# Interleaving two channels' lag weights in HBM, and making three of 32 chunks on chip instead of six

## The reference, cut to what matters

```python
# attention: r = layernorm(x); k = v = context
ek = exp(k)
A_t, B_t = sum over i<t of ew**(t-1-i) * ek_i * v_i, and the same without v   # ew = exp(w), per channel
#          the same again backwards, over i>t;  cur = exp(u + k)
wkv = (Af + Ab + cur * v) / (Bf + Bb + cur)
x = x + tanh(g_xattn) * sigmoid(r) * wkv
# feed-forward: z = layernorm(x), fake-quantised with one scale over all of z
h = fake_quant(silu(z @ quant(w_gate).T) * (z @ quant(w_up).T))
x = x + tanh(g_ffn) * h @ quant(w_down).T
```

## Time and profile before

| | |
|---|---|
| median of 3 timed runs | 212.69 us (212.09 to 212.9) |
| the profiled execution's own time | 211.43 us |
| its span, first to last instruction | 209.7 us |
| busy share of the span: PE, PEld | 82%, 60% |
| busy share: DVE, ACT, POOL | 80%, 75%, 66% |
| chunk products, line 1019 (PE) | 512 MATMUL, 60.4 us busy, 280 ns mean |
| DMA moved in all | 29.31 MB in 43328 packets |
| of these lag loads | 26 transfers of 512 KB, 7.3 us from issue to landing (median) |

### The profile page before, as it was taken

How to read it: one execution, slowest core, us unless ns; L and a number is a source line. 1 busy time by engine, 2 the same in 40 slices (tenths; PEclk the granted TensorE clock), 3 DMA queues, 4 the chain that set the end, 5 groups by cost and what they waited for, 6 DMA issues and landing times.

```text
span 209.7 us, 3447 instructions
## 1 busy us (share of the span) xinstructions
PE 172.9 (82%) x1146; PEld 125.8 (60%) x1146; DVE 166.8 (80%) x352; ACT 157.4 (75%) x242; POOL 138.7 (66%) x163
## 2 busy tenths in 40 slices
PE   4489996989899989988137987969889997789990
PEld 4456536989899989978126662324334432467780
DVE  0769586365755949999969968999799999889994
ACT  3459698737698699599879996958978891899910
POOL 3355223638869979986788852848897664058983
PEclk9969997899999999999855899999999999999998
DMA  3999999999999998500000000000000000025555
GB/s 89 331 375 348 349 328 292 296 283 297 278 292 319 243 250 216 159 28 2 0 0 0 0 3 2 0 0 0 0 3 0 0 0 2 3 76 171 171 185 200
DMA packets 43328, 29.31 MB, mean 140 GB/s; under 512 B 2224, under 2 KB 43056, under 8 KB 43312
## 3 DMA queue, kind: packets, MB, share of 16 engines
q1 hardware_dynamic: 42896, 28.58, 47.7%
q10 hardware_dynamic: 416, 0.52, 0.7%
HBM read 24.65 MB, written 4.46 MB: 139 GB/s over the span
## 4 chain that ended last, share of the span: by engine, by line
PE 34%; DVE 27%; ACT 17%; DMA 10%; issue 7%; POOL 3%; SPq 1%; DVEq 0%; ACTq 0%
PE ps L1019 10%; PE ps L1123 9%; DMA hidden<-lag_w 6%; PE ps L1159 5%; PE ps L1003 5%; DVE hidden L893 4%; DMA hidden<-in_ctx 4%; ACT hidden L551 3%; ACT z_t L702 2%; DVE hidden L911 2%; PE ps L1050 2%; DVE h_peaks L922 2%; ACT hidden L627 2%; ACT silu_out L681 2%; DVE z_t L964 2%
## 5 line engine op out<-in xcount | busy, mean ns | idle before, releaser
L1019 PE MATMUL ps<-hidden 128*128 128x128 f32 (+1 forms) x512 | 60.4, 280 | 6.0 <-DVE hidden L723 2.5
L1019 PEld LDWEIGHTS ps<-hidden 128*128 128x128 f32 x512 | 59.5, 196 | 7.4 <-issue 3.3
L922 DVE TENSOR_REDUCE h_peaks<-hidden (+2 forms) x24 | 26.0, 1122 | 2.0 <-POOL hidden L476 1.3
L418 POOL TENSOR_TENSOR x_all<-x_all,silu_out 128x512 f32<-128x512 f32 x15 | 22.9, 1542 | 6.3 <-DVE silu_out L792 6.3
L780 DVE SCALAR_TENSOR_TENSOR h_space<-z_t,ps 128x256 f32<-128x256 f32 x32 | 19.1, 598 | 8.6 <-PE ps L1019 8.2
L1159 PE MATMUL ps<-wdT,z_t 128*128 128x256 bf16 x192 | 22.6, 272 | 2.5 <-DVE z_t L964 2.3
L681 ACT ACTIVATE silu_out<-ps,mix_scale 128x1024 f32<-128x1024 f32 (+1 forms) x18 | 18.4, 1020 | 5.8 <-PE ps L1123 3.4
L1159 PEld LDWEIGHTS ps<-wdT,z_t 128*128 128x128 bf16 x192 | 17.6, 97 | 7.7 <-DVE z_t L964 2.9
L1043 PE MATMUL ps<-ident,hidden 128*128 128x128 f32 x64 | 11.6, 342 | 10.0 <-POOL hidden L457 8.5
L792 DVE SCALAR_TENSOR_TENSOR silu_out<-ps,small,silu_out 128x256 f32<-128x256 f32 x32 | 15.1, 476 | 5.5 <-ACT silu_out L532 3.4
L521 ACT ACTIVATE z_t<-x_all,mr,nr 128x256 f32<-128x256 f32 x32 | 16.4, 588 | 3.6 <-POOL mr L380 3.6
(11 more groups left out here) (116 smaller groups left out, 374.0 us busy)
## 6 DMA issues: line engine op xcount, KB each, us to landing
hidden<-lag_w SPq DMA_DIRECT2D x26, 512.0 KB, 7.3
x_all<-in_x SPq DMA_DIRECT2D x8, 512.0 KB, 8.9
hidden<-in_ctx SPq DMA_DIRECT2D x8, 512.0 KB, 9.1
out<-x_all SPq DMA_DIRECT2D x15, 256.0 KB, 2.1
xq<-in_L_ffn_w_down SPq DMA_DIRECT2D x1, 704.0 KB, 6.1
xq<-in_L_ffn_w_gate SPq DMA_DIRECT2D x1, 640.0 KB, 6.9
h_space<-in_L_ffn_w_up SPq DMA_DIRECT2D x1, 640.0 KB, 6.2
out<-x_all ACTq DMA_DIRECT2D x1, 256.0 KB, 2.4
```

The lines of the kernel that those rows point to most:

```text
L418: nc.gpsimd.tensor_tensor(xs, xs, mixed[:, m % 2, :, :].rearrange("p c b -> p b c"), ALU.add).then_inc(s["x1_done"], 1)
L922: nc.vector.tensor_reduce(h_peaks[:, bass.ds(KA * b + k, 1)], hidden[:, bass.ds(b * HB + k * BT, cols)], AX.X, ALU.max, apply_absolute_val ...
L1019: last = nc.tensor.matmul(ps[:, j % BANKS, c * 2 * SEQS:end * 2 * SEQS], lag_tile(j)[:, c, :], ekp[:, (j * CK + c) * 2 * SEQS:(j * CK + en ...
```

## The change

`SET = CG = 2`. The lag values now stand in HBM as (lag, channel of the pair), so that the two channels of a pair alternate. A partition's run for a pair of channels is 256 consecutive values, 1024 bytes, and a chunk's load has four such runs in each partition where it had eight of 512 bytes. In the ring tile the two channels of a pair alternate as well, so `lag_matrix(j, c)` of a loaded chunk is a view with a step of two elements (8 bytes). A made chunk keeps its former layout. MADE shrinks to 10, 14 and 18. `exp_clips` moves from step 12 to step 9 and `sigmoid_clips` from step 13 to step 10. The third transpose of weights moves from between chunks 30 and 31 to behind chunk 31.

```diff
+    SET = CG
-    MADE = 10, 14, 18, 22, 26, 30
+    MADE = 10, 14, 18
 def lag_tile(j):
-            return ring[(GROUPS + j) % SLOTS].rearrange("p (g t) -> p g t", t=T)
+            tile = ring[(GROUPS + j) % SLOTS]
+            if j in MADE:
+                return tile.rearrange("p (c t) -> p c t", t=T)
+            return tile.rearrange("p (g t i) -> p g i t", t=T, i=SET)
+        def lag_matrix(j, c):
+            return lag_tile(j)[:, c, :] if j in MADE else lag_tile(j)[:, c // SET, c % SET, :]
...
-        lag_w = up_out[:, 512:512 + CG * LAGS].rearrange("p (i j) -> p i j", i=CG)
+        lag_flat = up_out[:, 512:512 + CG * LAGS]
+        lag_w = lag_flat.rearrange("p (j i) -> p i j", i=CG)
...
-                src = bass.AP(lag_dram, j * CK * LAGS, [[1, P], [LAGS, CK], [1, T]])
-                sp.dma_start(lag_tile(j), src)
+                src = bass.AP(lag_dram, j * CK * LAGS, [[SET, P], [SET * LAGS, CK // SET], [1, SET * T]])
+                sp.dma_start(ring[(GROUPS + j) % SLOTS].rearrange("p (g n) -> p g n", n=SET * T), src)
...
-                act.dma_start(lag_dram[:, :], lag_w.rearrange("p i j -> p (i j)"))
+                act.dma_start(lag_dram[:, :], lag_flat)
...
-                if m == 12:
+                if m == 9:
                     exp_clips()
-                if m == 13:
+                if m == 10:
                     sigmoid_clips()
...
-                    last = nc.tensor.matmul(ps[...], lag_tile(j)[:, c, :],
+                    last = nc.tensor.matmul(ps[...], lag_matrix(j, c),
...
-                if j in (14, 23, 30):
-                    turn_weights((14, 23, 30).index(j))
+                if j in (14, 23):
+                    turn_weights((14, 23).index(j))
+            turn_weights(2)
```

More of the change, by code:

```diff
@@ L293, in load_lags @@
                     sp.wait_ge(s["ab_done"], before - GROUPS + 1)
-                src = bass.AP(lag_dram, j * CK * LAGS, [[1, P], [LAGS, CK], [1, T]])
-                sp.dma_start(lag_tile(j), src).then_inc(ring_in[(GROUPS + j) % SLOTS], 16)
+                src = bass.AP(lag_dram, j * CK * LAGS, [[SET, P], [SET * LAGS, CK // SET], [1, SET * T]])
+                sp.dma_start(ring[(GROUPS + j) % SLOTS].rearrange("p (g n) -> p g n", n=SET * T), src).then_inc(ring_in[(GROUPS + j) % SLOTS], 16)
             def load_weights(m):
@@ L508, in lag_weights @@
                 act.wait_ge(s["lag_done"], CG + 1)
-                act.dma_start(lag_dram[:, :], lag_w.rearrange("p i j -> p (i j)")).then_inc(s["lag_stored"], 16)
+                act.dma_start(lag_dram[:, :], lag_flat).then_inc(s["lag_stored"], 16)
             def exp_k(g):
@@ L1018, in accumulate @@
                     end = min(c + 2, CK)
-                    last = nc.tensor.matmul(ps[:, j % BANKS, c * 2 * SEQS:end * 2 * SEQS], lag_tile(j)[:, c, :],
+                    last = nc.tensor.matmul(ps[:, j % BANKS, c * 2 * SEQS:end * 2 * SEQS], lag_matrix(j, c),
                                             ekp[:, (j * CK + c) * 2 * SEQS:(j * CK + end) * 2 * SEQS], start=True, stop=True)
```

## The result

| | before | changed |
|---|---|---|
| first comparison, median | 212.66 us (212.09 to 212.9, 4 runs) | 210.0 us (209.42 to 211.26, 4 runs) |
| ratio, 95% interval | | 0.9887 [0.9838, 0.9936] |
| repeated later, median | 212.14 us (209.78 to 214.05, 23 runs) | 209.89 us (209.09 to 210.75, 12 runs) |
| ratio, 95% interval | | 0.9917 [0.9882, 0.9952] |

The change made the kernel faster by about 1%: 2.7 and 2.3 us by the medians, against 4.1 forecast. By the ratios, which leave out the few executions in a slower state, the gain is 2.4 and 1.8 us. 208.6 us was predicted and 210.0 measured. That is inside the range that should hold the time (206.8 to 211.0), but outside the forecast's own, narrower range (207.2 to 209.4).

A forecast was written before the change was run, and what follows sets the result against it. TensorE, over 90% filled in the chunks, was taken as the bound, with VectorE setting the end about as much. Gains of 1.65 and 2.7 us made 4.3, taken as 4.1: 212.69 - 4.1 = 208.6 us, range 206.8 to 211.0.

The forecast's parts named there:

- I am wrong if the pitch grows: Sign against the forecast: TensorE's pitch per matmul in the chunks rises above 0.113 to 0.115 us.
- rivals 1 and 2: Loads get no faster (210.0 us, chance 0.12); VectorE doesn't get its quick TENSOR_SCALARs (209.8 us, chance 0.17).
- Both waits for loads go: TensorE's load waits before chunks 6 and 11 (0.85 and 0.89 us) vanish with 1 KB rows; 1.65 us counted.
- Three more loads cost nothing: Loading chunks 22, 26 and 30 instead of making them: 0 counted, 2.6 us in all if late.
- The made chunks and VectorE beside an idle GpSimd: Three fewer made chunks save VectorE 1.2 us of waits; beside idle GpSimd, its TENSOR_SCALARs up to 2.8 us.
- The moved transpose: Third weight transpose behind chunk 31: TensorE saves 0.67 us wait and 0.68 us of transposes; costs nothing there.
- TensorE reads with a step of 8 bytes: I take 0: TensorE's reads of loaded chunks: the step costs 0; bounds were nothing or twice the pitch, +53 us.
- rival 3: Step of two slows TensorE's weight load: 220.8 us at 23%, 262 at 100%, decides from 8% of pitch; chance 0.10.
- The sum: Stage of the chunks: 2.7 us plus 1.65 of the first gaps make 4.3; 4.1 us taken.
- rival 1: Lag loads get no faster: 210.0 us, or 212 if three added loads each come 0.85 late; chance 0.12.
- What follows moves with the last mix: Statistics, layer norm and feed-forward after the chunks hang on the last mix, so the span shortens by 4.1 us.
- Rival 4: The change's time is given back after chunk 31, where TensorE's clock falls: half the gain, 210.7 us; chance 0.11.

The follow-up runs named there:

- experiment 5: Changed kernel with only the layout undone (rows of 512 bytes, no step, three made chunks); 209.72 us, ratio 0.9872 to the kernel before.
- experiment 10: Changed kernel with the third transpose of weights and the clip work back in their old places; 209.9 us, ratio 0.9888 to the kernel before.
- experiment 3: Changed kernel, but TensorE reads loaded tiles with a step of 4 elements (16 bytes) in place of 2; 262.15 us, ratio 1.2361 to the kernel before.
- experiment 9: Changed kernel with ten more unused GpSimd instructions where chunks 22, 26 and 30 were made; 211.56 us, ratio 0.9957 to the kernel before.
- experiment 7: Changed kernel, but chunks 19 to 31 loaded from a second HBM copy in 512-byte rows without a step; 209.66 us, ratio 0.9897 to before.

## Why the prediction was right, and where not

The measured time lies in the range, and most of the mechanism is as forecast, but the forecast gain of 4.1 us wasn't reached. The range held the time because it had been made wide for the rivals. By one of the prediction's own signs, "I am wrong if the pitch grows", its term for the step was wrong, and the measured time came nearer to that of rivals 1 and 2 (210.0 and 209.8), neither of which happened. That is chance.

- *Both waits for loads go*: right, but with little to spare. 330 GB/s was measured where 348 was taken, and without the long rows the waits return (2.5 us, experiment 5). In experiment 10, whose first chunks ran at full clock, 0.24 us of waiting for a load came back before chunk 6. Chunk 14, the next late one, waited 0.26 us there, where I had said 0.1.
- *Three more loads cost nothing*: right in the stage of the chunks, even with short rows. The longer tail below goes with them.
- *The made chunks and VectorE beside an idle GpSimd*: right in mechanism. The TENSOR_SCALARs shrank by 2.7 us (2.67 + 0.83 to 0.59 + 0.17), and GpSimd kept busy brings 2.15 of that back and 1.0 us of the stage. That VectorE and TensorE hold each other, so that such a gain counts only in part, was right too.
- *The moved transpose*: its 0.67 us are in the trace ahead of chunk 31, and the stage is longer by as much, but the times can't tell it.
- *TensorE reads with a step of 8 bytes: I take 0*. This is the term that failed. No row supported the 0; VectorE's reading at 1 KB, from which I argued, was no guide to TensorE's weight load: a step of 16 bytes already costs TensorE 107% (experiment 3), where 1 KB costs VectorE 23%. The step of 8 bytes measured 0.0061 us a product, 5%, which is 29 x 16 x 0.0061 = 2.8 us of TensorE and 1.9 us of the stage. Of rival 3 it is the mild form: below the 8% from which it would have decided, and more than a third of the forecast gain.
- *The sum*, 4.1: without the step the stage would be 68.35 - 63.39 = 5.0 us shorter at the same clock, TensorE's whole slack of 4.9 and more than the 4.1 that I counted. With it, it is 3.0. (A slip in rival 1: three loads late by 0.85 us each on top of 210.0 give 212.5, not 212.)
- *What follows moves with the last mix*: not wholly. The tail is 0.5 us longer in every trace with 29 lag loads (37.40 to 37.48) and not in the three with 26 (36.87 to 36.92). The last store takes 2.8 to 2.9 us to land instead of 2.4. The layout isn't the cause (short rows with 29 loads have it, long rows with 26 haven't), and neither is GpSimd's idleness (experiment 9 has it). What is remains open; I didn't try another number of transfers elsewhere.
- *Rival 4* (time given back after chunk 31, where the clock falls) can't be excluded. 3.0 - 0.5 = 2.5 us is left at the end, the medians say 2.7 and 2.3 and the ratios 2.4 and 1.8. The fall in gate/up, 1.5 us in seven of nine traces, is 1.2 us on average. If the kernel before never had it, 1.3 us would be left, less than all of these, though the second ratio's interval reaches down to 1.0. That it has the fall too is likelier, but not shown: there are two traces of it.

For the step, the Trainium skill ("SBUF — State Buffer", section Door 1) gave two accesses to a 16-byte line as enough and up to four f32 as a free step. The first half is nearly borne out (5% lost at two per line); the second is not, as a step of four more than doubled the pitch (0.234 us against 0.113), and the measurement decides. The Trainium skill's rule that 512 bytes reach line rate ("DMA: Bandwidth & Descriptors", section Specifications) differs from the trace as well: 296 GB/s in rows of 512 bytes against 330 in rows of 1 KB for the same lag data.

## What to carry to other kernels

Price the reader of a new layout together with its transfer. An interleave that makes HBM runs longer puts a step into every later read, and if the reader is the bound (PEld busy 5.00 of 5 us here), a few per cent of pitch eat what the transfer gave. Keeping the layout to the part where loads are late took 1.1 us off the stage in one trace (experiment 7), though the times couldn't tell it. And when work is taken off one engine, look at which instructions of its neighbour were slow only while it ran: here they made up 1.0 of the 1.9 us that the three made chunks cost.

## What the runs showed of the hardware that I had not expected

- TensorE loads f32 weights of 128 x 128 at a pitch of 0.113 us without a step, 0.118 to 0.119 with a step of 8 bytes, and 0.234 with one of 16 bytes (granted clock 1.00, and one MATMUL with each load).
- A partly low clock in the first chunks made this stage of the changed kernel 1.1 to 1.5 us longer. Idle products that held the clock gained nothing there, as in both traces with them chunk 1's load took 10.7 and 11.3 us to land, not 8.5 to 8.9; why is open.
- The landing time of the last store, 2.4 or 2.8 to 2.9 us, went with the number of lag loads more than 100 us earlier.
